# The first feed-forward chunks of a two-layer macaron block: scatters three chunks late, the gate sum on VectorE, new orders

## The chip, the cores and the metric

The kernel runs on one core of one Trainium2 chip. A core has five engines that work side by side, each through its own instructions in order: TensorE (PE in the rows: matrix products; PEld is its weight load), VectorE (DVE), ScalarE (ACT), GpSimd (POOL) and SyncE (SP, which here only issues transfers). They wait for each other on semaphores, and transfers (DMAs) run beside them. The metric is the device time of the program in microseconds (us), the median of three runs. A time is compared at 0.2%, some 4.1 us here.

## The reference, cut to what matters

```python
def _L0_ffn_ref(x, norm_weight, router_w, router_b, fc1_w, fc1_b, fc2_w, fc2_b):
    T, e = b * s, 8;  cap = T // e
    xn = x_flat * rsqrt(mean(x_flat * x_flat) + EPS) * norm_weight
    probs = softmax(xn @ router_w.T + router_b)
    gates, idx = top_k(probs.T, cap)            # every expert picks its cap rows
    hmid = gelu(einsum('ech,efh->ecf', xn[idx], fc1_w) + fc1_b)
    ye = einsum('ecf,ehf->ech', hmid, fc2_w) + fc2_b
    out = zeros.at[flat_idx].add(ye * gates)    # scatter, summed over experts
    gate_sums = zeros.at[flat_idx].add(gates)
    return out / maximum(gate_sums, 1e-9)
x = x + 0.5 * _L0_ffn_ref(_layernorm(x), ...)
x = x + _L0_attn_ref(_layernorm(x), ...)        # causal attention, one head
x = x + 0.5 * _L0_ffn_ref(_layernorm(x), ...)
```

x has 32 x 512 = 16384 rows of 256 numbers; there are 8 experts, each picks 2048 rows and has a hidden width of 1024. All is float32.

## The kernel before, in words

The program goes through router scores, a binary search for each expert's threshold, the first feed-forward layer (layer 0), attention, a second search and the second feed-forward layer (layer 1). Products are made of three float16 products each (`split3`), from a high half (`_h`, made by ScalarE) and a low half (`_l`, made by VectorE).

A feed-forward layer has 32 chunks n of 512 rows, four to an expert (c = n % 4). The text counts chunks from 0. A chunk passes these stations:

- GpSimd gathers its rows from memory (`gather`, four indirect DMAs, one for each block t of 128 rows), and gathers their gate weights (`weights`, four more).
- In layer 0 alone the rows must be normalised: VectorE takes statistics (`rows_stats`, ends in `cx`), GpSimd takes the root (`roots`, `zsx`), VectorE makes the shift (`rows_shift`, `zbx`), ScalarE writes the high half `xs` (`rows_hi`), VectorE the normalised row and the low half (`rows_lo`).
- SyncE turns them by DMA transposes into `xt` (`columns`).
- TensorE makes eight blocks f of the hidden layer (`fc1`, three PSUM banks in turn), ScalarE applies gelu and makes `hid_h`, VectorE `hid_l` (`hidden_lo`), TensorE makes four output blocks t (`fc2`), VectorE adds the bias (`y_bias`, `yb`), ScalarE multiplies by the gate weight (`y_out`, `ys`), and GpSimd adds them to memory by indirect DMAs (`scatter`).

All engines loop over steps m and quarters t. In step m TensorE alternates between two blocks of fc1 of chunk m and one block of fc2 of chunk m - 1. There is no scheduler: the order on each engine is the order of the code, and each engine waits in it. ScalarE in quarter 0 of step m makes two gelus, then `rows_hi(m + 1)`, then goes on with the third gelu, for which TensorE's sixth block (f = 5) waits.

In the first chunks of a layer VectorE still has the choice of rows for experts 1 to 7 to finish (`choice_1` to `choice_8`, in `first_turns`), GpSimd makes the gates and their sums over experts (`gate_sums`, `gates`), and SyncE stores them in memory (`gate_d`), from which `weights` gathers. TensorE makes two small products for the choice (`other_limits`, `other_places`), and a wait of TensorE for VectorE's `choice_7` stands in front of the second. The tables `scaled` and `scattered` say in which step a chunk's `y_out` and scatter stand: from step 5 on both handle chunk m - 1.

## Time and profile before

| | us |
|---|---|
| median of 3 runs | 2062.29 (2060.1 to 2063.11) |
| the profiled execution | 2063.0 |
| its span in the trace | 2061.1 |
| TensorE busy | 1961.4 (95%) |
| VectorE busy | 1452.7 (70%) |
| ScalarE busy | 1399.2 (68%) |
| GpSimd busy | 1260.2 (61%) |

The profiled execution's own time lies 1.9 us above its span and 0.7 us above the median. In a row of the timeline the number in brackets is how long the engine stood idle before the instruction, and behind the arrow is what ended the wait.

### The profile page before, as it was taken

The page shows a single profiled execution, that of the slowest core. Times are in us where ns is not written, and L with a number is a line of the kernel's source. Part 1 is how long each engine was busy: PE and PEld are TensorE (multiplying, and loading weights), DVE is VectorE, ACT ScalarE, POOL GpSimd, SP SyncE. Part 2 cuts the span into 40 slices and gives each one's busy share as a digit, 9 for nine tenths or more (in the row PEclk, how much of TensorE's full clock was granted, in tenths as well). Part 3 has the DMA queues.
Part 4 walks back from the last instruction along what each step waited for, and adds up shares of the span by engine and source line. Part 5 has one row for each costly group of instructions (what it writes and reads, how often), then busy time and mean ns, then how long its engine had stood idle before and what let it go on. Part 6 is the DMA issues. An engine that isn't in the chain of part 4 may idle for free. (4 is left out here: it accounts for less than half of the span.)

```text
span 2061.1 us, 42656 instructions
## 1 busy us (share of the span) xinstructions
PE 1961.4 (95%) x15442; PEld 1360.4 (66%) x15442; DVE 1452.7 (70%) x4301; ACT 1399.2 (68%) x2680; POOL 1260.2 (61%) x1438
## 2 busy tenths in 40 slices
PE   8858999999999999799999999779999999999997
PEld 6635666666666666577777777535666666666665
DVE  7788777677777765488899998787565555656542
ACT  8636666766767776578888787555676676676663
POOL 8234877777777776644444442027877676767674
PEclk9979999999999999999999999989999999999999
DMA  9943555646465544556555553234655464646442
GB/s 289 349 128 93 116 95 96 103 91 131 85 109 93 101 71 70 118 126 160 159 160 164 136 150 109 93 82 104 108 119 100 92 107 88 132 85 108 70 79 35
DMA packets 361746, 242.34 MB, mean 118 GB/s; under 512 B 228929, under 2 KB 348993, under 8 KB 361281
## 3 DMA queue, kind: packets, MB, share of 16 engines
q1 hardware_dynamic: 304192, 172.34, 31.8%
q0 software_dynamic: 57344, 67.29, 21.6%
q8 instruction: 122, 2.00, 0.4%
q14 instruction: 88, 0.71, 0.1%
HBM read 121.03 MB, written 84.93 MB: 100 GB/s over the span
## 5 line engine op out<-in xcount | busy, mean ns | idle before, releaser
L1272 DVE SCALAR_TENSOR_TENSOR hid_l<-hf,hid_h 128x512 f16<-128x512 f32 x512 | 352.4, 700 | 339.8 <-ACT hid_h L718 338.5
L1493 PE MATMUL ps<-w_h,hid_h 128*128 128x256 f16 x2048 | 559.5, 273 | 0.0
L1494 PE MATMUL ps<-w_l,hid_h 128*128 128x256 f16 x2048 | 559.4, 273 | 0.0
L1495 PE MATMUL ps<-w_h,hid_l 128*128 128x256 f16 x2048 | 559.3, 273 | 0.0
L1493 PE MATMUL ps<-xt,w_h 128*128 128x512 f16 x1024 | 390.6, 381 | 16.8 <-ACT hf L819 15.5
L819 ACT ACTIVATE hf<-ps,b 128x512 f32<-128x512 f32 x512 | 345.4, 675 | 75.7 <-PE ps L1495 69.3
L1495 PE MATMUL ps<-xt,w_l 128*128 128x512 f16 x1024 | 390.6, 381 | 0.0
L1494 PE MATMUL ps<-xt,w_h 128*128 128x512 f16 x1024 | 390.5, 381 | 0.0
L718 ACT ACTIVATE ys<-yb,weight 128x256 f32<-128x256 f32 x256 | 128.0, 506 | 340.6 <-DVE yb L1290 335.6
L718 ACT ACTIVATE hid_h<-hf 128x512 f16<-128x512 f32 x512 | 322.5, 630 | 16.3
L605 POOL DMA_INDIRECT weight<-gate_d,gate_at x256 | 258.2, 1009 | 84.0 <-issue 76.8
L615 POOL DMA_INDIRECT out<-ys,tok x128 | 206.7, 1615 | 112.9 <-ACT ys L718 80.3
L1493 PEld LDWEIGHTS ps<-w_h,hid_h 128*128 128x128 f16 x2048 | 201.0, 98 | 50.7 <-issue 0.8
L1494 PEld LDWEIGHTS ps<-w_l,hid_h 128*128 128x128 f16 x2048 | 200.9, 98 | 50.5 <-issue 0.8
L615 POOL DMA_INDIRECT x_d<-ys,tok x128 | 206.7, 1615 | 37.4 <-issue 36.7
L1495 PEld LDWEIGHTS ps<-w_h,hid_l 128*128 128x128 f16 x2048 | 200.8, 98 | 23.5
L595 POOL DMA_INDIRECT xe<-z_d,tok x128 | 138.1, 1079 | 90.6 <-issue 90.3
L595 POOL DMA_INDIRECT xe<-x,tok x128 | 132.4, 1034 | 99.2 <-DVE gate_at L1227 61.2
L1495 PEld LDWEIGHTS ps<-xt,w_l 128*128 128x128 f16 x1024 | 100.7, 98 | 122.3 <-issue 2.8
L1493 PEld LDWEIGHTS ps<-xt,w_h 128*128 128x128 f16 x1024 | 100.7, 98 | 114.0 <-ACT hf L819 17.5
L1494 PEld LDWEIGHTS ps<-xt,w_h 128*128 128x128 f16 x1024 | 100.6, 98 | 94.3 <-issue 1.9
L1290 DVE TENSOR_TENSOR yb<-ps,b_now 128x256 f32<-128x256 f32 x256 | 107.6, 420 | 62.1 <-PE ps L1495 61.1
(292 smaller groups left out, 3848.7 us busy)
## 6 DMA issues: line engine op xcount, KB each, us to landing
w_st<-fc_t SPq DMA_DIRECT2D x32, 1024.0 KB, 6.3
xin<-x SPq DMA_DIRECT2D x32, 512.0 KB, 5.6
xa<-x_d SPq DMA_DIRECT2D x32, 512.0 KB, 4.5
out<-x SPq DMA_DIRECT2D x32, 512.0 KB, 5.2
z_d<-z SPq DMA_DIRECT2D x32, 512.0 KB, 6.0
xt<-xs SPq DMA_TRANSPOSE x256
weight<-gate_d,gate_at POOLq DMA_INDIRECT x256, 2.8
b_st<-fc_b SPq DMA_DIRECT2D x16, 128.0 KB, 5.7
```

What stands on the lines that cost most here:

```text
L595: pool.indirect_dma_start(xe[:, n % 2, t, :], None, rows, bass.IndirectOffsetOnAxis(ap=tok[:, E % 3, k:k + 1].bitcast(U32), axis=0)).then_ ...
L605: pool.indirect_dma_start(weight[:, E % 3, k:k + 1], None, gate_d, bass.IndirectOffsetOnAxis(ap=gate_at[:, E % 3, k:k + 1].bitcast(U32), a ...
L615: pool.indirect_dma_start(acc, bass.IndirectOffsetOnAxis(ap=tok[:, E % 3, k:k + 1].bitcast(U32), axis=0), ys[:, n % 2, t, :], None, comput ...
L718: return act.activation(dst, src, ACT.Copy, **kw)
L819: act.activation(hf[:, f % HF, :], bank(FC1[f % 3]), ACT.Gelu, bias=b1[:, e, f:f + 1], scale=1.0 / WS).then_inc(s_gelu, 1)
L1272: dve.scalar_tensor_tensor(hid_l[:, n % 2, f, :], hf[:, f % HF, :], HS, hid_h[:, n % 2, f, :], ALU.mult, ALU.subtract).then_inc(s_hl, 1)
L1290: dve.tensor_tensor(yb[:, n % 2, t, :], bank(4 + t % 2)[:, 0:D], b2_now[:, n // NC % 2], ALU.add).then_inc(s_yb, 1)
L1493: pe.matmul(dst, lh, rh, start=first, stop=False)
L1494: pe.matmul(dst, lh, rl, start=False, stop=False)
L1495: return pe.matmul(dst, ll, rh, start=False, stop=last)
```

## The change

- SyncE: expert 1's `w2_in` is issued before the gates are stored, and the store moves behind it.
- GpSimd: the four additions of the gate sum go; the product `gate = equal * p_r` stays (`chosen`). The order of gathers, roots, weights and scatters of the first chunks is another. The scatter of chunk n comes four steps late (n = m - 4), from step 13 on three, from step 18 on two, from step 24 on one; so steps 12, 17 and 23 hold two scatters each. `weights` of chunk m - 1 stands in step m (before: of chunk m).
- VectorE: sums the gates over experts by one reduction (`gate_scale`), which reads `gate` with a step of 128 numbers. The parts of the choice, the statistics and the count of slots stand in other places; from step 4 on `rows_stats(m + 2)` stands in quarter 2, not 3.
- ScalarE: in chunks 2 and 3 of layer 0 it writes the normalised row as well (`NORMED`), and VectorE's copy of that work goes. `y_out` handles chunk m - 2 until step 22, two chunks in step 23, then m - 1.
- The halves of the attention's weights are made within the first search (ScalarE rounds 6 to 9, VectorE rounds 8, 10, 11 and 13), no longer in the first chunks.
- The output buffer `ys` has four places instead of two (the new two lie where `above` and `scan` of the choice are).
- TensorE: `pick(E0, 3)` moves from step 1 to step 0, `other_limits` from quarter 0 to quarter 1 of step 1.

The diff, cut:

```diff
+    YS_RING = 4
+    LOWS = (8, 10, 11, 13)
+    NORMED = (2, 3)
...
+        LATE = 23
+
         def scaled(m, t):
...
+            if m < 3:
+                return []
+            if m in (3, LATE):
+                two = 2 * (t % 2)
+                return [((0 if m == 3 else m - 2) + t // 2, two), ((0 if m == 3 else m - 2) + t // 2, two + 1)]
+            return [(m - 2, t)] if m < LATE else [(m - 1, t)]
+
+        def weighted(m):
+
+            return [m - 1] if m < LATE - 3 else [m - 1, m] if m == LATE - 3 else [m]
 
         def scattered(m):
 
-            return {2: [0], 3: [1], 4: [2, 3]}.get(m, [m - 1])
+            lag = 4 if m < 13 else 3 if m < 18 else 2 if m <= LATE else 1
+            return [m - lag, m - lag + 1] if m in (12, 17, LATE) else [m - lag]
...
-                sp.wait_ge(s_gate, layer + 1)
-                sp.dma_start(gate_d..., gate[:, :, :]).then_inc(s_gate_d, 16)
                 w2_in(E0 + 1)
                 for m in range(1, LAST):
                     n, ahead = N0 + m, (N0 + m) // NC + 2
+                    if m == 2:
+                        sp.wait_ge(s_gate, layer + 1)
+                        sp.dma_start(gate_d..., gate[:, :, :]).then_inc(s_gate_d, 16)
...
-                roots(N0 + 2)
-                gate_sums(layer)
                 gather(N0 + 3)
+                chosen(layer)
+                roots(N0 + 3)
                 gates(layer)
-                roots(N0 + 3)
+                gather(N0 + 4)
                 pool.wait_ge(s_gate_d, 16 * (layer + 1))
                 weights(N0)
+                roots(N0 + 4)
                 weights(N0 + 1)
+                gather(N0 + 5)
+                weights(N0 + 2)
+                roots(N0 + 5)
...
-                for m in range(2, LAST + 1):
+                for m in range(4, LAST + 1):
                     if m + 2 < LAST:
                         gather(N0 + m + 2)
+                    late = m >= 12
+                    if not late:
+                        for n in scattered(m):
+                            scatter(N0 + n)
+                        if m + 2 < LAST:
+                            roots(N0 + m + 2)
+                    for n in weighted(m):
+                        if n < LAST:
+                            weights(N0 + n)
+                    if late and m + 2 < LAST:
                         roots(N0 + m + 2)
...
-                            act.activation(xs[:, t, 0, :], xe[:, n % 2, t, :], ACT.Identity, ...)
+                            for dst in (xs[:, t, 0, :], xe[:, n % 2, t, :])[0:2 if n in NORMED else 1]:
+                                last = act.activation(dst, xe[:, n % 2, t, :], ACT.Identity, ...)
...
-                link(dve.tensor_scalar(ginv[:, :], gsum[:, 0, :], 1e-9, None, ALU.max))
+                link(dve.tensor_reduce(ginv[:, :], gate[:, :, :].rearrange("p e t -> p t e"), AX.X, ALU.add))
+                link(dve.tensor_scalar(ginv[:, :], ginv[:, :], 1e-9, None, ALU.max))
...
-                    if (m, t) == (0, 0):
+                    if (m, t) == (0, 1):
+                        choice_2(layer)
+                    if (m, t) == (0, 3):
                         choice_3(layer)
-                    if (m, t) == (0, 2):
                         choice_4(layer)
                     if (m, t) == (1, 0):
+                        count_slots(0, E0, 3)
+                    if (m, t) == (1, 1):
                         choice_5(layer)
-                    if (m, t) == (1, 1):
                         choice_6(layer)
...
                     if (m, t) == (1, 2):
                         choice_7(layer)
+                        rows_stats(E0 * NC + 3)
...
-                        if t == 3 and m + 2 < LAST:
+                        if t == (3 if m < NC else 2) and m + 2 < LAST and m != 1:
                             rows_stats(n + 2)
```

SyncE, from chunk 1's transposes to chunk 3's in layer 0 (and the same in layer 1). `w_st` of L413 is expert 1's second weight matrix, `gate_d` the stored gates. Before:

```order
L420 DMA_TRANSPOSE xt<-xs 128x4x128 x8
L408 DMA w_st<-fc_t 128x2x1024
L420 DMA_TRANSPOSE xt<-xs 128x4x128 x4
L434 DMA gate_d<-gate 128x8x128
L413 DMA w_st<-fc_t 128x8x256
L414 DMA b_st<-fc_b 128x256
L420 DMA_TRANSPOSE xt<-xs 128x4x128 x4
```

The same place in the changed kernel, where L430 is the load of the second matrix and L455 the store:

```order
L437 DMA_TRANSPOSE xt<-xs 128x4x128 x8
L425 DMA w_st<-fc_t 128x2x1024
L437 DMA_TRANSPOSE xt<-xs 128x4x128 x4
L430 DMA w_st<-fc_t 128x8x256
L431 DMA b_st<-fc_b 128x256
L455 DMA gate_d<-gate 128x8x128
L437 DMA_TRANSPOSE xt<-xs 128x4x128 x4
```

The load of the second matrix has moved ahead of the store, which waits for the gates.

GpSimd in layer 0, from the first product of the gates to chunk 5's roots. `xe` rows are gathers, `weight` rows the gathers of gate weights, `zsx` the roots, `x_d<-ys` the scatters. Before:

```order
L571 TENSOR_TENSOR gate<-equal,p_r 128x1024
L572 TENSOR_TENSOR gsum<-gate 128x512
L575 TENSOR_TENSOR gsum<-gsum 128x256
L577 TENSOR_TENSOR gsum<-gsum 128x128
L595 DMA xe<-x,tok 128x256 x4
L581 TENSOR_TENSOR gate<-gate,ginv 128x1024
L622 TENSOR_TENSOR zsx<-cx,minus_half 128x4
L605 DMA weight<-gate_d,gate_at 128x1 x8
L595 DMA xe<-x,tok 128x256 x4
L605 DMA weight<-gate_d,gate_at 128x1 x4
L622 TENSOR_TENSOR zsx<-cx,minus_half 128x4
L615 DMA x_d<-ys,tok 16384x256 x4
```

In the changed kernel, from chunk 3's gather on:

```order
L607 DMA xe<-x,tok 128x256 x4
L589 TENSOR_TENSOR gate<-equal,p_r 128x1024
L634 TENSOR_TENSOR zsx<-cx,minus_half 128x4
L593 TENSOR_TENSOR gate<-gate,ginv 128x1024
L607 DMA xe<-x,tok 128x256 x4
L617 DMA weight<-gate_d,gate_at 128x1 x4
L634 TENSOR_TENSOR zsx<-cx,minus_half 128x4
L617 DMA weight<-gate_d,gate_at 128x1 x4
L607 DMA xe<-x,tok 128x256 x4
L617 DMA weight<-gate_d,gate_at 128x1 x4
L634 TENSOR_TENSOR zsx<-cx,minus_half 128x4
L607 DMA xe<-x,tok 128x256 x4
```

Chunk 3's gather now stands ahead of the product, the three rows of sums are gone, and no scatter stands in this stretch.

GpSimd in layer 0, where the lag of the scatters first shrinks (step 12). Before, a step like every other:

```order
L595 DMA xe<-x,tok 128x256 x4
L605 DMA weight<-gate_d,gate_at 128x1 x4
L622 TENSOR_TENSOR zsx<-cx,minus_half 128x4
L615 DMA x_d<-ys,tok 16384x256 x4
L595 DMA xe<-x,tok 128x256 x4
```

In the changed kernel:

```order
L607 DMA xe<-x,tok 128x256 x4
L617 DMA weight<-gate_d,gate_at 128x1 x4
L634 TENSOR_TENSOR zsx<-cx,minus_half 128x4
L627 DMA x_d<-ys,tok 16384x256 x8
L607 DMA xe<-x,tok 128x256 x4
```

Eight scatter DMAs instead of four stand ahead of the next chunk's gather; this is so again in steps 17 and 23.

## Rows read from the trace of the kernel before

**Rows 1.** Windows: length, busy PE, PEld, DVE, ACT, POOL; PEclk, DMA, GB/s.
```profile
187.59:214.48 26.89, 23.13 (x154) 15.11 (x154) 22.17 (x58) 14.75 (x26) 18.93 (x17) 0.94 0.52 151
214.48:235.77 21.29, 21.29 (x155) 14.52 (x153) 16.84 (x56) 14.65 (x27) 17.38 (x15) 1.00 0.55 86
235.77:263.88 28.11, 23.33 (x154) 14.72 (x152) 18.37 (x59) 14.80 (x27) 22.84 (x19) 0.94 0.52 107
1400.37:1429.16 28.79, 23.99 (x154) 15.46 (x154) 20.57 (x44) 14.00 (x26) 19.29 (x17) 0.88 0.56 147
```

**Rows 2.** Timeline of TensorE where it restarts: start, length, instruction, [idle before <-releaser].
```profile
187.34 0.39 PE L1627 MATMUL ps<-per_expert,before 128*128 128x7 f32 x2 [1.44 <-DVE per_expert L1181]
...
203.44 0.39 PE L1493 MATMUL ps<-xt,w_h 128*128 128x512 f16 x1 [3.76 <-ACT hf L819]
...
251.94 0.61 PE L1493 MATMUL ps<-xt,w_h 128*128 128x512 f16 x1 [3.48 <-ACT hf L819]
...
1417.27 0.61 PE L1493 MATMUL ps<-xt,w_h 128*128 128x512 f16 x1 [4.80 <-ACT hf L819]
```

**Rows 3.** Timeline of ScalarE before those restarts.
```profile
197.92 2.08 ACT L810 ACTIVATE xs<-xe,zbx,zsx 128x256 f16<-128x256 f32 x4 [6.20 <-DVE zbx L1258]
...
249.23 2.08 ACT L810 ACTIVATE xs<-xe,zbx,zsx 128x256 f16<-128x256 f32 x4 [8.53 <-DVE zbx L1258]
...
1416.01 0.63 ACT L718 ACTIVATE w_h<-w_st 128x512 f16<-128x512 f32 x1 [7.66 <-DMA w_st<-fc_t]
```

**Rows 4.** Timeline of SyncE's queue in layer 1.
```profile
1408.33 0.37 SPq L434 DMA_DIRECT2D gate_d<-gate  x1
```

**Rows 5.** Timeline of GpSimd in step 3 of layer 0: chunk 5's roots.
```profile
247.32 1.62 POOL L622 TENSOR_TENSOR zsx<-cx,minus_half 128x4 f32<-128x4 f32 x1
```

**Rows 6.** Timeline of VectorE in the first search and in steps 0 to 2.
```profile
103.71 0.29 DVE L1105 TENSOR_REDUCE got<-ps 128x2 f32<-128x128 f32 x1 [0.36 <-PE ps L1593]
...
145.92 0.75 DVE L979 SCALAR_TENSOR_TENSOR g_l<-ps,g_h 128x256 f16<-128x256 f32 x2
...
170.95 1.89 DVE L1264 TENSOR_SCALAR xe<-xe,zsx,zbx 128x256 f32<-128x256 f32 x4 [0.73 <-ACT xs L810]
...
194.11 1.41 DVE L1247 BATCH_NORM_STATS2 bstx<-xe 128x6 f32<-128x256 f32 x4 [1.39 <-DMA xe<-x,tok]
...
197.66 0.16 DVE L1258 SCALAR_TENSOR_TENSOR zbx<-mvx,zsx 128x4 f32<-128x4 f32 x1
```

**Rows 7.** Groups by line, VectorE's reductions: out<-in, shapes xcount | busy us, mean ns | idle before.
```profile
L1162 DVE TENSOR_REDUCE per_expert<-above 128x7 f32<-128x896 f32 x2 | 2.2, 1079 | 0.0
```

**Rows 8.** Groups by line, GpSimd, 300 to 800 us (24 steps of layer 0).
```profile
L615 POOL DMA_INDIRECT x_d<-ys,tok x96 | 153.8, 1602 | 26.8 <-issue 26.8
L595 POOL DMA_INDIRECT xe<-x,tok x94 | 97.2, 1034 | 28.6 <-issue 28.6
L605 POOL DMA_INDIRECT weight<-gate_d,gate_at x96 | 97.1, 1012 | 29.2 <-issue 29.2
L622 POOL TENSOR_TENSOR zsx<-cx,minus_half 128x4 f32<-128x4 f32 x24 | 27.2, 1135 | 41.9 <-DVE cx L1252 41.9
```

**Rows 9.** Transfers: issues by line, median us from issue to landing.
```profile
weight<-gate_d,gate_at POOLq DMA_INDIRECT x256, 2.8
...
xe<-x,tok POOLq DMA_INDIRECT x128, 2.9
```

**Rows 10.** Timelines of one undisturbed step of layer 0, which begins at 348.14.
```profile
348.14 0.38 PE L1493 MATMUL ps<-xt,w_h 128*128 128x512 f16 x1
...
354.99 2.06 ACT L810 ACTIVATE xs<-xe,zbx,zsx 128x256 f16<-128x256 f32 x4
...
360.08 0.38 PE L1493 MATMUL ps<-xt,w_h 128*128 128x512 f16 x1
...
365.29 0.42 DVE L1290 TENSOR_TENSOR yb<-ps,b_now 128x256 f32<-128x256 f32 x1
...
368.76 0.69 DVE L1272 SCALAR_TENSOR_TENSOR hid_l<-hf,hid_h 128x512 f16<-128x512 f32 x1 [0.55 <-ACT hid_h L718]
```

More of the change, by code:

```diff
@@ L189, in macaron @@
         p_r = sb("p_r", [P, NE, P], F32, ffn)
-        above = sb("above", [P, NE, P], F32, ffn)
         equal = sb("equal", [P, NE, P], F32, ffn)
-        scan = sb("scan", [P, NE, P], F32, ffn)
+        choice = ExitStack()
+        above = sb("above", [P, NE, P], F32, choice)
+        scan = sb("scan", [P, NE, P], F32, choice)
+        choice.close()
+        ys_more = sb("ys_more", [P, 2, TG, D], F32, ffn)
         w1_h = sb("w1_h", [P, 2, KD, FF], F16, ffn)
@@ L297, in macaron @@
         s_xe = [sem("s_xe0"), sem("s_xe1")]
-        s_sc = [sem("s_sc0"), sem("s_sc1")]
+        s_sc = [sem(f"s_sc{u}") for u in range(YS_RING)]
         s_xt = [sem("s_xt0"), sem("s_xt1")]
@@ L665, in ffn_rows @@
                         scatter(m - 1, 2, TG)
-                    else:
-                        for n in scattered(m)[len(early):]:
+                    elif late:
+                        for n in scattered(m):
                             scatter(N0 + n)
@@ L706, in _ @@
             ffn_rows(1, z_d, outf)
-            for u in range(2):
-                pool.wait_ge(s_sc[u], 16 * TG * NC * NE)
+            for u in range(YS_RING):
+                pool.wait_ge(s_sc[u], 16 * TG * (2 * NC * NE // YS_RING))
             pool.sem_inc(s_phase, 1)
@@ L724, in _, with attention_weights @@
             last.then_inc(s_split, 1)
-            def attention_weights():
-                act.wait_ge(s_gm, 2 * KD)
-                for n, dst in enumerate((g_h, m_h)):
-                    for k in range(KD):
-                        last = copy(dst[:, k, :], bank(4 + n)[:, k * D:(k + 1) * D], scale=WS)
-                last.then_inc(s_gmh, 1)
+            def attention_weights(n, k):
+                act.wait_ge(s_gm, KD * (n + 1))
+                copy((g_h, m_h)[n][:, k, :], bank(4 + n)[:, k * D:(k + 1) * D], scale=WS).then_inc(s_gmh, 1)
             def high(g, k):
@@ L773, in route @@
                         act.activation(junk_a[:, :], key, ACT.Sign, bias=at[:, 2:3], scale=-1.0, accum_out=signs[:, 2:3]).then_inc(s_signs, 1)
+                    if layer == 0 and 6 <= i < 6 + 2 * KD:
+                        attention_weights((i - 6) // KD, (i - 6) % KD)
                     if i == 2:
@@ L850, in ffn @@
                     w2_hi(E0, h)
-                if layer == 0:
-                    attention_weights()
                 rows_hi(N0)
@@ L1102, in route @@
                             router_columns(rounds // 3 - 1)
+                        if layer == 0 and rounds in LOWS:
+                            attention_weights(LOWS.index(rounds) // KD, LOWS.index(rounds) % KD)
                         rounds += 1
@@ L1220, in count_slots @@
                 if q == 0:
-                    for u in range(2):
-                        wait(dve, s_sc[u], 16 * TG * (NC // 2) * (E - 2))
+                    for u in range(YS_RING):
+                        wait(dve, s_sc[u], 16 * TG * (NC // YS_RING) * (E - 2))
                     for c in range(NC):
@@ L1260, in rows_lo @@
                 def rows_lo(n, t0=0, t1=TG):
-                    if layer == 0:
+                    if layer == 0 and n not in NORMED:
                         for t in range(t0, t1):
@@ L1333, in ffn @@
                     w1_lo(E0, 1)
+                b2_rows(E0)
                 rows_shift(N0, 2, TG)
-                if layer == 0:
-                    b2_rows(E0)
                 rows_lo(N0, 2, TG)
-                if layer == 1:
-                    b2_rows(E0)
+                count_slots(0, E0, 2)
                 choice_1(layer)
-                count_slots(0, E0, 2)
-                if layer == 0:
-                    router_halves()
-                    attention_weights()
-                choice_2(layer)
-                for h in range(4):
+                w2_lo(E0, 0)
+                rows_stats(N0 + 1)
+                for h in range(1, 4):
                     w2_lo(E0, h)
-                rows_stats(N0 + 1)
                 for m in range(LAST + 1):
@@ L1689, in ffn @@
                             pick(ahead, 2 * c + t // 2)
[L1690 removed]
+                        if (m, t) == (0, 3):
+                            pick(E0, 3)
+                        if (m, t) == (1, 1):
                             other_limits(layer)
[L1692 removed]
                         if (m, t) == (1, 3):
```

63 lines of the change are left out of this document (23 added, 40 removed).

## The prediction, made before the changed kernel was run

> **What bounds the kernel now.** I first read the busy rows of the page: TensorE works 95% of the span, so a change can win only where it stands still or runs at its lower clock. The windows of single chunks show where [rows 1]: a normal step with two `pick` products takes 21.29 us at a granted clock of 1.00 and TensorE is busy throughout. In layer 0 step 2 takes 26.89 us and step 4 takes 28.11; in layer 1 step 2 takes 28.79. These three steps lose 5.60, 6.82 and 7.50 us. The timeline of TensorE gives the stall inside each: 3.76, 3.48 and 4.80 us, all released by a gelu of ScalarE [rows 2]; the remainder is the clock, granted at 0.94, 0.94 and 0.88 of full in those windows, so at the lower level, 1.2 GHz, for some us after each stall. The first matmul after the last two stalls takes 0.61 us where one at full clock takes 0.38 [rows 2, 10]. A shorter stall of 1.44 us stands at the end of step 1, for VectorE's `choice_7` [rows 2].
>
> The timeline of ScalarE says what the gelu stood behind [rows 3]. In layer 0 step 2, `rows_hi(3)` waited 6.20 us for VectorE's shift. In step 4, `rows_hi(5)` waited 8.53 for a shift whose root GpSimd made at 247.32, behind chunk 1's scatters [rows 5]. In layer 1 step 2, the copy of expert 1's second matrix waited 7.66 us for its load, which SyncE issues only behind the store of the gates at 1408.33 [rows 4].
>
> **The change, part by part.** *Layer 1.* The load now stands ahead of the store and is free to go when chunk 2's transposes are out, in step 1, almost a step earlier, which covers a wait of 7.66 us with room. What is late next is `rows_hi(3)`: its gather now goes out ahead of the product of the gates and the sums, so it has landed. Weights of chunk 0 come after the store and after chunk 4's gather, but `y_out(0)` now stands in step 3 and not at the end of step 2, 20 us later. So the 7.50 us go whole. `other_places` finds `choice_7` done there. Gain: 7.5 us.
>
> *Layer 0, step 4.* Chunk 5's root no longer has a scatter ahead of it, since the first scatter stands in step 4 behind chunk 6's gather. VectorE ends chunk 5's statistics at about the time its quarter 3 ends, 1 us of root follows, and the shift is there about 7.5 us into step 4, before `rows_hi(5)` and 2 us before TensorE would want the third gelu (TensorE's f = 5 begins at 360.08 - 348.14 = 11.9 us into a step [rows 10]). Of the 6.82 us I leave 0.5, for a `pick` whose tiles VectorE makes no earlier than now. Gain: 6.3 us.
>
> *Layer 0, steps 0 to 2.* Here VectorE sets the pace, and it works in order. It sheds the four low halves of the attention's weights, 2 x 0.75 us less the overlap, 1.3 us [rows 6], and chunk 3's statistics no longer wait 1.39 us for a gather [rows 6]. It sheds chunk 2's normalisation, 1.89 us and a wait of 0.73 [rows 6], but gains nothing by that: the low halves of chunk 2 now wait for ScalarE, which makes eight activations at 2.08 / 4 = 0.52 us each [rows 3], 4.2 us in all, and the old pair of passes took about as long. It takes on the sum of 1024 numbers. The nearest row is a reduction of 896 contiguous numbers, 1.08 us [rows 7], so 1.2 us if the step costs nothing, 2.4 if every element costs two; I take 1.2, by the row. The choice's parts now all lie before chunk 2's statistics, which gives back about 0.5. Chunk 3's shift, at 197.66 before [rows 6], comes 1.39 + 1.3 - 1.2 - 0.5 = 1.0 us earlier; `rows_hi(3)` itself takes twice as long (4.2 for 2.08), and the load of the matrix, which ended the stall before, is no longer in the way. TensorE's restart, 203.44 [rows 2], moves to about 202.6: 0.8 us. Its idle time there is still some 3 us, between the 1.44 of step 1 and the 3.48 after which the matmul took 0.61, so the lower clock goes or stays: 5.60 - 3.76 = 1.8 us, of which I take 0.8. Steps 0 to 2 then give 1.6 us, with ends of 0 and 4 (the 1.44 of step 1 may grow, since TensorE gets there sooner than VectorE).
>
> The Trainium skill speaks against this sum (SBUF — State Buffer, "Door 1: The DMA port swizzle"): reads that go to a new 16-byte line with each element pay a penalty, and here the step is 512 bytes. It gives no figure for VectorE. By the rows the sum is 1.2 us; by the rule it is longer, up to the 2.4 taken as the end above, which would leave 0 to 0.4 us of step 2's gain. No row of this kernel has such a step in SBUF, so the trace neither agrees nor disagrees.
>
> *The search.* Each of the four rounds gets one low half of 0.4 us on VectorE, which waits 0.36 us for TensorE in a round [rows 6]. Cost: 0.1 us or less a round, 0.2 in all; at worst 1.6.
>
> *The catch-up steps of layer 0.* This is what the change adds. GpSimd's work in a step is 4 x (1.60 + 0.28) = 7.5 us of scatters, 4 x (1.03 + 0.30) = 5.3 of gathers, 4 x (1.01 + 0.30) = 5.3 of weights and 1.1 of roots [rows 8]: 19.2 of 20.9 to 21.3 us, and it waited 41.9 us for `cx` in 24 steps, 1.75 a step [rows 8], which is the same slack. In steps 12, 17 and 23 eight scatters, 15 us, stand between chunk m + 2's root and chunk m + 3's gather. Times from the start of a step: `yb` of quarter 2 begins at 365.29 - 348.14 = 17.2 [rows 10] and statistics now follow it, 17.6 to 19.6; the root ends at 20.7. Fifteen us of scatters bring GpSimd to 36, the fourth gather is issued at 36 + 3 x 1.33 = 40.1 and lands 2.9 us later [rows 9], at 43.0, which is 22.1 us into the next step. VectorE wants it at 17.6, and waits 4.5 us in front of its last two low halves of the hidden layer. They normally end at 368.76 + 0.69 = 369.45, as the following step begins [rows 10], and fc2 of that chunk needs them after two blocks of fc1, 2.6 us later. Now the statistics end at 24.1 and the two low halves at 25.5, which is 4.6 into the following step. TensorE stands for 2.0 us. With 1.75 us of slack a step the queue has recovered before the next catch-up. Three of them: 6.0 us lost, with ends of 0 (the wait is swallowed) and 10 (3.5 each, with a clock that falls). In layer 1 there are no statistics, gathers run a step ahead, and nothing is lost.
>
> *The weights one step late.* From step 4 to 11 the weights of chunk m - 1 go out behind the root, from 20.9, land at 20.9 + 3 x 1.31 + 2.8 = 27.6, 6.7 us into the next step [rows 8, 9]. There `y_out` waits for them in front of `rows_hi`, which then ends at 6.7 + 0.4 + 2.1 = 9.2, and the third gelu at 9.9, TensorE wants it at 11.9. Before, `rows_hi` began at 354.99 - 348.14 = 6.9 [rows 10], so this costs ScalarE half a us and TensorE nothing. If it came 2 us later than I reckon, it would cost from there on in each of eight steps.
>
> The sum: 7.5 + 6.3 + 1.6 - 0.2 - 6.0 = 9.2 us. The profiled execution's 2063.0 us becomes 2053.8, and the median, 0.7 below it, 2053.1.
>
> **The rivals.** *The catch-ups cost nothing.* If VectorE's wait is shorter than its slack (scatters overlap more tightly than their mean, or the gather lands sooner), the 6.0 us stay: 2047.1. For it: the slack of 2.6 us is more than half of the wait. Against it: the arithmetic has 15 us in front of a gather that had 7.5.
>
> *Only SyncE's move pays.* VectorE stays the bound of layer 0's first chunks, the strided sum takes 2.4 us, the lower clock stays, and catch-ups and late shifts take back what step 4 gives: 7.5 - 2.5 = 5 us, 2057.3. For it: VectorE was busy 22.17 of 26.89 us in step 2, which leaves little [rows 1].
>
> *GpSimd's queue becomes the bound of layer 0.* Place: steps 4 to 22 of layer 0, the loop cx, root, weights, `y_out`, `rows_hi`, third gelu. It decides from the point where the weights land 2 us later than reckoned, for example when scatters at four steps' lag meet gathers in the transfer queues and a step of GpSimd grows from 19.2 to over 21 us. At 2 us beyond that point, eight steps cost 16 us, and 16 - 9.2 = 7 us are lost: 2069. For it: GpSimd's slack is 1.75 us a step and the slack of the gelu 2.0. Against it: the work of a step is the same as before.
>
> *It does not do what it says.* The waits are there but another one ends at the same time (the transposes, the ring of four `hf` tiles): within 2 us of before, 2061.
>
> **How the numbers follow.** Forecast 2053.1 with 0.42, its own range 2050 to 2057. Catch-ups free 0.24 (2047.1), only the load 0.18 (2057.3), GpSimd's queue the bound 0.09 (2069), nothing gained 0.07 (2061). The range that holds the time 8 times in 10 takes in the first three: 2045.5 to 2060.5. A measurement of this kernel tells 0.2%, 4.1 us, from no change. Faster by more than that (under 2058.2): the first two and two thirds of the third, 0.78. Within it: a third of the third and the last, 0.14. Slower: 0.08.
>
> **What would show it.** In layer 1, step 2 should take 21.3 us with no wait of ScalarE for `w_st`. In layer 0, step 4 should take under 22 us; step 2 about 25 to 26, with a wait for `zbx` still in it; and the timeline of VectorE should show waits of 3 to 5 us for `xe` in steps 13, 18 and 24, each with a stall of TensorE of about 2 us released by `hid_l`. The reduction into `ginv` should take 1.2 us. Wrong it would be if steps 5 to 12 are longer than 20.9 to 21.3 us, or if TensorE stands still at a place that this text does not name.

## The result, and the profile after

| | before | after |
|---|---|---|
| median, 20 runs each | 2062.24 us (2059.19 to 2067.44) | 2067.96 us (2064.89 to 2072.9) |
| profiled execution, its span | 2063.0, 2061.1 | 2065.61, 2063.5 |
| GpSimd busy | 1260.2 us | 1275.5 us |

The changed kernel is slower: ratio 1.0028, 95% interval 1.0022 to 1.0034. Its profiled execution was one of its quickest (2065.61 against a median of 2067.96), so the two traces differ by 2.4 us where the medians differ by 5.7. The traces account for those 2.4.

The windows of single steps, columns as in [rows 1]: layer 0's steps 2, 8, 14, 19 and 25, and layer 1's step 2.

```profile
186.61:216.03 29.42, 23.88 (x155) 15.00 (x154) 24.52 (x55) 16.06 (x28) 12.00 (x9) 0.88 0.30 88
322.22:344.99 22.77, 21.45 (x154) 14.46 (x152) 16.96 (x48) 13.61 (x24) 15.72 (x13) 1.00 0.66 123
452.18:476.89 24.71, 22.69 (x147) 14.82 (x145) 18.64 (x54) 16.33 (x29) 20.12 (x18) 0.93 0.54 109
561.14:584.03 22.89, 21.01 (x146) 14.00 (x144) 16.03 (x44) 13.88 (x24) 18.64 (x16) 1.00 0.43 72
689.57:713.55 23.98, 21.47 (x155) 14.45 (x153) 17.07 (x62) 14.68 (x25) 19.17 (x17) 1.00 0.42 75
1409.21:1430.71 21.50, 21.45 (x155) 14.44 (x154) 20.91 (x44) 13.53 (x24) 8.32 (x6) 1.00 0.40 73
```

Two of the three long steps of [rows 1] are gone: layer 1's step 2 takes 21.50 us (28.79 before), layer 0's step 4 takes 21.93 (28.11). Step 2 of layer 0 got longer, 29.42 for 26.89. Steps 8, 14, 19 and 25, which took 21.29, 20.84, 20.84 and 21.29 before, have become long.

The timeline of TensorE after, its restarts in those steps and in step 12; one later matmul shows the clock.

```profile
204.58 0.61 PE L1513 MATMUL ps<-xt,w_h 128*128 128x512 f16 x1 [5.41 <-ACT hf L842]
339.56 0.38 PE L1686 MATMUL ps<-counts,tile_of 128*128 128x128 f16 x4 [1.32 <-DVE tok_f L1240]
425.46 0.38 PE L1686 MATMUL ps<-counts,tile_of 128*128 128x128 f16 x4 [1.49 <-DVE tok_f L1240]
456.96 0.28 PE L1513 MATMUL ps<-w_h,hid_h 128*128 128x256 f16 x1 [2.02 <-DVE hid_l L1294]
461.06 0.57 PE L1513 MATMUL ps<-xt,w_h 128*128 128x512 f16 x1
565.77 0.28 PE L1513 MATMUL ps<-w_h,hid_h 128*128 128x256 f16 x1 [1.88 <-DVE hid_l L1294]
694.84 0.28 PE L1513 MATMUL ps<-w_h,hid_h 128*128 128x256 f16 x1 [2.51 <-DVE hid_l L1294]
```

Three causes stand behind these rows. *Steps 14, 19, 25*: VectorE waits for the gather that stands behind eight scatters, in steps 13, 18 and 24.

```profile
453.62 1.41 DVE L1269 BATCH_NORM_STATS2 bstx<-xe 128x6 f32<-128x256 f32 x4 [6.25 <-DMA xe<-x,tok]
562.50 1.41 DVE L1269 BATCH_NORM_STATS2 bstx<-xe 128x6 f32<-128x256 f32 x4 [5.94 <-DMA xe<-x,tok]
691.56 1.41 DVE L1269 BATCH_NORM_STATS2 bstx<-xe 128x6 f32<-128x256 f32 x4 [5.18 <-DMA xe<-x,tok]
```

*Steps 8 and 12*: the weights land late, so ScalarE (first row, step 8) makes the high half late, VectorE (second row) waits for it, and everything behind it on VectorE is late, last `tok_f`, which TensorE's `pick` waits for.

```profile
329.86 0.51 ACT L740 ACTIVATE ys_more<-yb,weight 128x256 f32<-128x256 f32 x1 [3.50 <-DMA weight<-gate_d,gate_at]
330.89 1.89 DVE L1286 TENSOR_SCALAR xe<-xe,zsx,zbx 128x256 f32<-128x256 f32 x4 [2.77 <-ACT xs L832]
```

*Step 2*: VectorE's timeline, and GpSimd's two products beside it. The last row is chunk 3's shift.

```profile
181.66 4.25 DVE L1200 TENSOR_TENSOR_SCAN scan<-equal 128x896 f32<-128x896 f32 x1
192.13 1.90 DVE L1215 TENSOR_REDUCE ginv<-gate 128x128 f32<-128x1024 f32 x1
195.46 3.44 DVE L1294 SCALAR_TENSOR_TENSOR hid_l<-hf,hid_h 128x512 f16<-128x512 f32 x2
199.16 0.14 DVE L1280 SCALAR_TENSOR_TENSOR zbx<-mvx,zsx 128x4 f32<-128x4 f32 x1
```

```profile
181.65 2.36 POOL L589 TENSOR_TENSOR gate<-equal,p_r 128x1024 f32<-128x1024 f32 x1
195.63 2.73 POOL L593 TENSOR_TENSOR gate<-gate,ginv 128x1024 f32<-128x1024 f32 x1 [5.89 <-DVE ginv L1218]
```

The shift was at 197.66 [rows 6] and the step began 0.98 later than now, so within the step it is 2.5 us later. The scan took 2.21 us before, and the two low halves in this place 1.28:

```profile
196.05 1.28 DVE L1272 SCALAR_TENSOR_TENSOR hid_l<-hf,hid_h 128x512 f16<-128x512 f32 x2
```

Step by step from the starts of the fc1 blocks, the account of the traces (gain positive): all ahead of layer 0's first fc1, the search included, +0.85; step 0 +2.28; step 1 -2.15; step 2 -2.53; step 4 +6.18; steps 8 and 12 -1.48 and -1.65; steps 14, 19, 25 -3.87, -2.05, -2.69; step 28 -0.39; from the start of layer 0's last chunk to the fc1 of layer 1 (attention and the second search lie there) -1.78; layer 1's steps 0 and 1 together +0.44, step 2 +7.29; from the start of its last chunk to the end -0.85. Sum -2.4.

### The profile page after: what moved, and what is told of

Its sections match the earlier page's. It is cut to its first block, busy times and chain, and to the rows that moved or that the text cites. A ratio compares the mean times of both kernels' runs of the same rounds, so it can differ in the third digit from the quotient of the medians.

```text
span 2063.5 us, 42662 instructions
## 1 busy us (share of the span) xinstructions
PE 1958.3 (95%) x15442; PEld 1357.8 (66%) x15442; DVE 1453.5 (70%) x4295; ACT 1403.1 (68%) x2688; POOL 1275.5 (62%) x1432
## 4 chain that ended last, share of the span: by engine, by line
PE 65%; POOL 12%; issue 9%; DVE 7%; ACT 4%; DMA 2%; SPq 1%; DVEq 0%; POOLq 0%; ACTq 0%
PE ps L1513 20%; PE ps L1515 20%; PE ps L1514 20%; POOL x_d L627 5%; POOL xe L607 3%; POOL weight L617 2%; ACT zt_l L740 2%; PE ps L1739 1%; ACT zt_h L740 1%; PE ps L1613 1%; DVE hid_l L1294 1%; POOL zsx L634 1%; DMA xe<-x,tok 1%; DVE bst L1023 1%; PE ps L1768 1%
## 5 line engine op out<-in xcount | busy, mean ns | idle before, releaser
L607 POOL DMA_INDIRECT xe<-x,tok x128 | 136.7, 1068 | 112.6 <-DVE gate_at L1249 75.3
L627 POOL DMA_INDIRECT out<-ys,tok x64 | 108.1, 1689 | 44.9 <-issue 31.4
L627 POOL DMA_INDIRECT out<-ys_more,tok x64 | 104.9, 1639 | 42.5 <-ACT ys_more L740 26.0
L561 POOL TENSOR_TENSOR nt<-mv,minus_one 128x4 f32<-128x4 f32 x64 | 13.4, 210 | 184.9 <-DVE mv L1027 184.9
```

The lines of the kernel that those rows point to most:

```text
L607: pool.indirect_dma_start(xe[:, n % 2, t, :], None, rows, bass.IndirectOffsetOnAxis(ap=tok[:, E % 3, k:k + 1].bitcast(U32), axis=0)).then_ ...
L627: pool.indirect_dma_start(acc, bass.IndirectOffsetOnAxis(ap=tok[:, E % 3, k:k + 1].bitcast(U32), axis=0), scaled_rows(n)[:, t, :], None, c ...
```

## The experiments

Each kernel was timed beside the kernel before, with 4 to 12 executions of it; e_flat alone has a single one. Line numbers in rows are those of the kernel named. What a step took beyond its undisturbed 21.29 or 20.84 us, from the starts of the fc1 blocks in each trace, steps 2 to 30 of both layers, under 0.2 us left out. A step is read from one execution of each kernel, and that one can be among its quickest or slowest (the ratio is from all of them). Steps 0 and 1 are not in the table: step 1 of layer 0 takes 23.3 us in before, a_load, b_root, x_ring, x_root and y_chosen, and 25.0 to 27.0 in the others.

| kernel | layer 0: step and us lost | layer 1 | ratio to before (95%) |
|---|---|---|---|
| before | 2: 5.6, 4: 6.8 | 2: 7.5 | 1 |
| after | 2: 8.1, 4: 0.6, 8: 1.5, 12: 1.6, 14: 3.9, 19: 2.1, 25: 2.7, 28: 0.4 | 2: 0.2 | 1.0028 (1.0022 to 1.0034) |
| a_load | 2: 4.8, 4: 6.9 | 2: 0.6, 5: 7.7 | 1.0008 (0.9999 to 1.0018) |
| b_root | 2: 5.9, 4: 0.7, 5: 5.1, 8: 4.4 | 2: 7.0, 5: 1.3 | 1.0015 (1.0006 to 1.0024) |
| f_two | 2: 6.4, 4: 0.7, 5: 6.4 | 2: 0.6, 5: 7.7 | 1.001 (1.0001 to 1.0019) |
| x_ring | 2: 6.6, 4: 0.7, 5: 4.3 | 2: 0.6, 6: 1.4 | 0.998 (0.997 to 0.9989) |
| x_root | 2: 6.6, 4: 0.7, 6: 4.9, 10: 0.3, 20: 4.3 | 2: 0.6, 6: 2.0 | 0.9977 (0.9967 to 0.9986) |
| c_catch | 2: 7.5, 4: 0.7, 8: 1.5, 12: 1.7, 15: 6.0, 20 to 26: 4.7, 28: 0.4 | 2: 0.2 | 1.0025 (1.0012 to 1.0038) |
| d_weights | 2: 8.6, 4: 0.7, 14: 4.4, 19: 4.1, 25: 4.3 | 2: 0.2 | 1.0021 (1.0012 to 1.003) |
| s_spread | 2: 7.7, 4: 0.7, 8: 0.9, 12: 2.2 | 2: 0.2 | 0.9981 (0.9972 to 0.999) |
| e_scale | 2: 12.6, 3: 2.8, 4: 0.6, 8, 12: 3.1, 14, 19, 25: 9.7 | 2: 8.1, 3: 1.9 | 1.012 (1.0105 to 1.0136) |
| g_scale | 2: 2.0, 4: 0.7, 8, 12: 3.2, 14, 19, 25: 9.8, 28: 0.3 | 2: 0.8 | 1.0004 (0.9992 to 1.0015) |
| t_all | 2: 12.6, 3: 2.7, 4: 0.6, 23: 0.7, 28: 0.4 | 2: 8.1, 3: 1.9 | 1.0035 (1.0023 to 1.0047) |
| w_best | 2: 2.0, 3: 0.8, 28: 0.6 | 2: 0.8 | 0.9931 (0.9919 to 0.9944) |
| y_chosen | 2: 3.9, 4: 0.6, 28: 0.2 | 2: 0.8 | 0.9931 (0.9918 to 0.9944) |

### Parts of the change put into the kernel before

**a_load.**

```diff
                 columns(N0 + 2)
-                sp.wait_ge(s_gate, layer + 1)
-                sp.dma_start(gate_d..., gate...).then_inc(s_gate_d, 16)
                 w2_in(E0 + 1)
                 for m in range(1, LAST):
...
+                    if m == 2:
+                        sp.wait_ge(s_gate, layer + 1)
+                        sp.dma_start(gate_d..., gate...).then_inc(s_gate_d, 16)
```

> The kernel before with one edit: in both layers SyncE issues the load of expert 1's second matrix ahead of the store of the gates, and the store stands where the changed kernel has it. My theory: this alone is worth what layer 1's step 2 lost, 7.5 us, so 2054.7 us (ratio to before 0.9964); step 2 of layer 1 takes about 21.5 us and ScalarE has no wait for w_st. Rival: in the kernel before chunk 3's gather still stands behind the gate sums on GpSimd, and a wait for it or for weight takes the place of the one removed: 2 to 4 us gained only, 2059, and step 2 at 25 us. Layer 0 gains nothing in either.

Measured 2064.55 us: nothing gained. Step 2 of layer 1 lost only 0.6, as both theories of its own step allow, but step 5 took 28.96 us. ScalarE's and TensorE's rows there:

```profile
1478.31 0.51 ACT L719 ACTIVATE ys<-yb,weight 128x256 f32<-128x256 f32 x1 [10.14 <-DMA out<-ys,tok]
1480.67 0.61 PE L1494 MATMUL ps<-xt,w_h 128*128 128x512 f16 x1 [4.69 <-ACT hf L820]
```

ScalarE waits 10.14 us for a buffer that a scatter still reads. In this trace and in that of before GpSimd works from 1413 to 1489 with no pause but the 0.3 us between two issues. So the scatters of chunk 2, for which ScalarE waits, are out only 2.6 us sooner (the last is issued at 1474.51, before at 1477.10), while TensorE begins step 5 at 1463.88 instead of 1471.74. Without the stall of step 2 TensorE comes to them sooner than they are done: there the stall had been the time in which GpSimd drew level. Neither theory had this.

**b_root.**

```diff
-                    early = scattered(m)[:1] if m in (3, 4) else []
+                    early = scattered(m)[:1] if m == 4 else []
```

> The kernel before with one edit: in step 3 GpSimd makes chunk 5's root ahead of chunk 1's scatters, not behind them; ring of two output buffers, everything else as before. My theory: step 4 of layer 0 (28.11 us) falls to 22 to 23, 5 to 6 us gained, ratio 0.9973, and the four output buffers and the three-step lag were not needed for it. Rival: with two buffers the scaling of chunk 3 waits for chunk 1's scatters, now 1.4 us later, and the stall of step 4 stays in another place: 0 to 2 us gained, ratio 0.9995.

Measured 2065.86 us. Step 4 fell to 22.00 us, as the theory has it, and step 5 rose to 26.39 and step 8 to 25.67, so nothing is gained: the rival's wait for a scatter came, a step later than it said. In step 5 a root behind the next scatters (VectorE waits 5.22 us for it) and a scatter behind them are late together; in step 8 ScalarE waits 4.74 us for weights. ScalarE and TensorE in step 5:

```profile
269.60 0.51 ACT L718 ACTIVATE ys<-yb,weight 128x256 f32<-128x256 f32 x1 [8.39 <-DMA x_d<-ys,tok]
272.70 0.61 PE L1493 MATMUL ps<-xt,w_h 128*128 128x512 f16 x1 [3.53 <-ACT hf L819]
```

**f_two** has both edits.

> The kernel before with both small moves, SyncE's load ahead of the store and chunk 5's root ahead of chunk 1's scatters, ring of two. Theory (GpSimd's backlog): the stalls come back as they did with each move alone, in step 5 and 8 of layer 0 (5.1 and 4.4 us) and step 5 of layer 1 (7.7 us), so nothing is gained: ratio 1.000 to 1.002. Rival: the two moves together gain what each took out of its own step, 6 + 7, ratio 0.994.

Measured 2064.86 us. Step 5 of layer 1 loses the same 7.7 us, step 5 of layer 0 loses 6.4, step 8 nothing: the first theory holds but for step 8.

**x_ring** is f_two with `YS_RING = 4` and `scaled_rows` taken over from the change, `scaled` and `scattered` left alone.

> As f_two, and four output buffers in place of two, with scaling and scatters where the kernel before has them (no lag, no catch-up). Theory: with two buffers ScalarE waits 8 to 10 us for a scatter in step 5; four buffers take that wait away, so step 5 of both layers is 21.3 us and the gain stays: layer 1 gives 7, layer 0 gives 6, less up to 4.4 in step 8 where ScalarE waits for weight: ratio 0.994 to 0.9965. Rival: GpSimd is late by its own work, and the next thing behind it (root, gather or weight) is late by as much in steps 5 to 8 whatever the ring: ratio 0.999 to 1.001.

Measured 2057.89 us, a ratio between those of theory and rival. Layer 1 is as the theory has it: step 5 takes 21.28 us, and only 1.4 come back, in step 6. In layer 0 step 5 still takes 25.54, and the wait there is not for a scatter now. VectorE's row:

```profile
268.81 0.16 DVE L1267 SCALAR_TENSOR_TENSOR zbx<-mvx,zsx 128x4 f32<-128x4 f32 x1 [5.79 <-POOL zsx L631]
```

**x_root** sets `early = []` as well, so that every root stands ahead of the scatters.

> As x_ring, and chunk 6's root too ahead of the scatter of step 4, so that in every step the root stands ahead of the scatters; scaling and scatters are as early as in the kernel before. Theory: what stayed in x_ring (step 5 of layer 0 at 25.5 us) is VectorE's wait of 5.8 us for that root, behind chunk 2's scatters; it goes, and step 5 is 21.3 us: 4.2 us less than x_ring, 2053.7, ratio to before 0.996. Then neither the lag of three steps nor the catching up was needed. Rival: GpSimd's own backlog still makes gathers or weights late in steps 5 to 8, at least 3 of the 4 us come back there: ratio 0.9975 or more.

Measured 2059.33 us. Step 5 takes 21.29, and step 6 takes 25.73: the wait is now VectorE's, for a gather.

```profile
286.85 1.41 DVE L1256 BATCH_NORM_STATS2 bstx<-xe 128x6 f32<-128x256 f32 x4 [5.65 <-DMA xe<-x,tok]
```

The rival holds. This trace, that of the slowest of the kernel's 11 executions, also has a stall of TensorE of 2.47 us in step 20 that x_ring's lacks: ScalarE waits 4.67 us there for weights, and `tok_f` is late behind it; why the weights came late is open. With prompt scatters GpSimd's backlog costs 4 to 7 us somewhere in steps 4 to 6 of layer 0 (before, b_root, f_two, x_ring, x_root), whichever wait is moved. In the changed kernel, with its lag, steps 5 to 7 are undisturbed, and they stay so in g_scale and w_best, below, where step 2 no longer gives GpSimd time. Up to and with its work for step 4 GpSimd makes the scatters of four chunks in the kernel before and of one in the changed kernel, some 22 us less. This speaks for the lag, but no run takes the lag alone out of the change or puts it alone into the kernel before; the sums that GpSimd sheds and its new order could have a share.

### Parts of the change taken back or mended

**c_catch.**

```diff
-                    if m + 2 < LAST:
+                    if m + 2 < LAST and len(scattered(m - 1)) == 1:
                         gather(N0 + m + 2)
...
                         for n in scattered(m):
                             scatter(N0 + n)
+                            if len(scattered(m)) == 2 and n == scattered(m)[0]:
+                                gather(N0 + m + 3)
```

> The changed kernel with one edit: in steps 12, 17 and 23 the gather of chunk m + 3 stands between the two scatters and not behind both. My theory: the waits of VectorE for xe in steps 13, 18 and 24 (6.25 us in step 13) and the stalls of TensorE behind them (2.02, 1.88, 2.51 us and the lower clock after the first) go; steps 14, 19 and 25 of the changed kernel are 3.9, 2.1 and 2.7 us too long, so 7.5 to 8.5 us come back: ratio to before 0.9989 (after: 1.0028). Rival: eight scatters fill GpSimd for 15 us wherever the gather stands, so weights or scatters are late instead, and only a third comes back: 1.0015.

Measured 2068.84 us, no better than the changed kernel. Step 14 is undisturbed and step 15 loses 6.0:

```profile
475.66 1.41 DVE L1271 BATCH_NORM_STATS2 bstx<-xe 128x6 f32<-128x256 f32 x4 [6.92 <-DMA xe<-x,tok]
478.93 0.40 PE L1515 MATMUL ps<-w_h,hid_h 128*128 128x256 f16 x1 [2.85 <-DVE hid_l L1296]
```

The gather after the one I had saved was late. The rival's reason holds (eight scatters are too much for a step), and not even its third came back.

**s_spread.**

```diff
+        EXTRA = (8, 13, 23)
...
         def scattered(m):
-            lag = 4 if m < 13 else 3 if m < 18 else 2 if m <= LATE else 1
-            return [m - lag, m - lag + 1] if m in (12, 17, LATE) else [m - lag]
+            def quarters(m):
+                return TG * (m - 3) + sum(min(max(m - a + 1, 0), TG) for a in EXTRA)
+            return [divmod(q, TG) for q in range(quarters(m - 1) if m > 4 else 0, quarters(m))]
...
-                        for n in scattered(m):
-                            scatter(N0 + n)
+                        for n, t in scattered(m):
+                            scatter(N0 + n, t, t + 1)
```

> The changed kernel with one edit: GpSimd makes up the three steps of lag not with eight scatters in each of steps 12, 17 and 23, but with one tile's scatter more in each of steps 8 to 11, 13 to 16 and 23 to 26. Theory: a step of GpSimd has about 1.75 us free and one more scatter is 1.9 us, so the queue stays within a fraction of a us; the waits for xe and the stalls of steps 13, 14, 19 and 25 go and with them 8.6 us (3.9 + 2.1 + 2.7), ratio to before 0.9986; steps 8 and 12 keep their 1.5 and 1.65. Rival: GpSimd is full anyway, so four steps with 1.9 us more each bring the same stall once at their end: 1.0015 or worse.

Measured 2059.14 us, ratio 0.9981 where the changed kernel has 1.0028. Steps 13 to 27 are all undisturbed. VectorE still waits for `xe` in several of them, 2.25 us at most, and its slack hides that. The trace is that of the quickest of 11 executions, 5.7 us under their median, so a typical one may lose more than it shows; the ratio, from all of them, gives a gain of 9.7 us.

**d_weights** makes `weights(m - 1)` stand ahead of `scatter(m - 4)` in layer 0's steps 4 to 11.

> The changed kernel with one edit: in layer 0, steps 4 to 11, GpSimd asks for the weights ahead of the scatters and not behind the root. My theory: steps 8 and 12 of the changed kernel are 1.5 and 1.65 us too long because ScalarE waits 3.5 and 3.9 us for weight, VectorE waits 2.8 and 3.2 for ScalarE's halves and makes the tiles late; these waits go and 3.1 us come back: ratio 1.0013. Rival: the root now stands at the end of the queue and comes later, so that the shift is late and steps 5 to 12 are all longer: 1.003 or more. Second rival: the tiles are late because the statistics stand in quarter 2, and nothing changes: 1.0028.

Measured 2066.03 us. Steps 8 and 12 take 21.28 and 21.29 us: the cause is as said, and both rivals are out. But steps 14, 19 and 25 lost 12.8 us here and 8.6 in the trace of after, with stalls that differ little (2.56, 2.25 and 2.43 us for 2.02, 1.88 and 2.51): the windows of the three steps show a clock of 0.93 each, where those of after show 0.93, 1.00 and 1.00. By the ratios 1.4 us of the 3.1 remain, which this measurement cannot tell from nothing.

**e_flat** changes only what is added up: `rearrange("p (t e) -> p t e")`.

> The changed kernel, with the reduction into ginv over 8 neighbouring numbers of the tile in place of numbers 128 apart (so the gates are divided by another sum; nothing else differs). It prices the stride: the strided one takes 1.90 us in the changed kernel. If the stride costs, it falls to about 1.2 us; if 128 short sums cost what they do whatever the stride, it stays at 1.9.

```profile
192.36 1.21 DVE L1215 TENSOR_REDUCE ginv<-gate 128x128 f32<-128x1024 f32 x1
```

So the stride costs 0.7 us of the 1.90 (in layer 1 the two take 1.21 and 1.94). By the Trainium skill (SBUF — State Buffer, "Door 1: The DMA port swizzle") each access that crosses to a new 16-byte line pays a penalty; these two rows agree in direction. Step 2 did not get shorter for it (29.46 us). Otherwise this kernel does in time what the changed one does, and it shows how far one execution is from another: steps 14 to 25 lose 13.2 us in its trace, 8.6 in that of after.

**e_scale.**

```diff
                     if (m, t) == (1, 3):
...
-                        gate_scale(layer)
...
+                    if (m, t) == (2, 1):
+                        gate_scale(layer)
```

> The changed kernel with one edit: VectorE makes the sums and the reciprocals of the gates (gate_scale) not at the end of step 1 but in step 2 behind chunk 3's shift and low halves. Theory: VectorE's order up to chunk 3's shift sets the restart of TensorE in step 2. 3.3 us of gate_scale and 2.2 us by which GpSimd's product stretched the low halves of the hidden layer go from in front of it: step 2 falls from 29.4 to 22.5 to 24.5 us, 5 to 7 us gained, ratio 0.9998. Rival: GpSimd is what bounds layer 0 from here, so a shorter step 2 only brings a wait for weight or scatter in steps 3 to 5: less than 2 us gained, 1.0022.

Measured 2086.57 us, my worst miss here. The shift came at 194.54, earlier as planned. But GpSimd could begin the product with `ginv` only at 209.17, and SyncE sends chunk 3's transposes behind the store of the gates. Rows of SyncE, then TensorE:

```profile
212.51 0.37 SPq L455 DMA_DIRECT2D gate_d<-gate  x1
212.97 5.89 SPq L437 DMA_TRANSPOSE xt<-xs  x4
```

```profile
221.35 0.61 PE L1514 MATMUL ps<-xt,w_h 128*128 128x512 f16 x1 [11.86 <-DMA xt<-xs]
```

**g_scale** puts it between the shift and the low halves instead.

```diff
                     if (m, t) == (1, 3):
...
-                        gate_scale(layer)
...
                             rows_shift(n + 1)
+                            if m == 2:
+                                gate_scale(layer)
                             rows_lo(n + 1)
```

> The changed kernel with one edit: gate_scale between chunk 3's shift and its low halves in step 2 (the edit of w_best alone). Theory: what the change lost in steps 0 to 2 is VectorE's order: 3.3 us of gate_scale and the 2.2 us by which GpSimd's product stretches the low halves of the hidden layer stand in front of chunk 3's shift. Step 2 falls from 29.4 to 23.3 us as in w_best, the rest of the changed kernel stays (steps 8, 12, 14, 19, 25 too long): 6 us less than the changed kernel, ratio to before 0.9999. Rival: a step 2 that is 6 us shorter gives GpSimd 6 us less before the weights of steps 5 to 12 and the first catching up, so steps 8, 12 and 14 grow by 3 us or more in all: ratio 1.0014 or more.

Measured 2062.95 us, 5.0 below the changed kernel. Step 2 takes 23.31 us. Steps 8, 12, 14, 19 and 25 lose 13.0 where they lost 11.7. The theory holds, and by the ratios this one place is worth 5.0 of the 5.8 us between the two kernels (the interval of g_scale's ratio is 2.4 us to either side).

**t_all** joins s_spread, d_weights and e_scale.

> The changed kernel with three edits together: scatters spread (as s_spread), weights ahead of the scatters in layer 0's steps 4 to 11 (as d_weights), gate_scale behind chunk 3's shift (as e_scale). If the three causes are separate, the gains add: 8.6 + 3.1 + 6 = 17.7 us from 2068, so 2050, ratio to before 0.9942. If GpSimd's queue is the common bound, the stalls move: 2058 to 2062, ratio 0.998 to 1.000, with a stall of TensorE in steps 3 to 6 or at the end of the spread.

Measured 2069.71 us; neither expectation came true, since both took e_scale for a gain. It carries e_scale's fault (12.6 and 2.7 us in steps 2 and 3, 8.1 and 1.9 in layer 1). Of steps 5 to 30 only 23 and 28 are disturbed, by 0.7 and 0.4 us.

**w_best** joins s_spread, d_weights and g_scale.

> The changed kernel with three edits: scatters spread (s_spread), weights ahead of the scatters in layer 0's steps 4 to 11 (d_weights), and gate_scale between chunk 3's shift and its low halves, so that GpSimd and SyncE get the gates at about the time they do now. Theory: s_spread's 2059.1, less 0.9 and 2.2 for steps 8 and 12, less 4.5 to 6 for step 2 (29.0 us there, 23 to 24.5 here): 2050.5, ratio 0.9943. Rival: the gates are again late at GpSimd or at SyncE and chunk 3's transposes wait behind the store: step 2 or 3 as long as before or longer, ratio 0.997 or more.

Measured 2047.81 us (2045.67 to 2052.05), ratio 0.9931, interval 0.9919 to 0.9944: 14.8 us below the kernel before and, by the ratios, 20 below the changed one. It also beats the theory's 2050.5. Its VectorE at chunk 3's shift:

```profile
193.24 0.15 DVE L1287 SCALAR_TENSOR_TENSOR zbx<-mvx,zsx 128x4 f32<-128x4 f32 x1
193.31 1.92 DVE L1222 TENSOR_REDUCE ginv<-gate 128x128 f32<-128x1024 f32 x1
196.65 3.58 DVE L1297 TENSOR_TENSOR xs<-xe,xs 128x256 f16<-128x256 f32 x4
```

**y_chosen** is w_best with `roots(N0 + 3)` ahead of `chosen(layer)`.

> w_best with one edit more: GpSimd makes chunk 3's root ahead of the product of the gates, so that the product no longer runs beside VectorE's scan (4.25 us in the changed kernel, 2.21 in the kernel before). Theory: the scan falls to 2.2 us and the stall of 2.19 us at the end of step 1 with it; 1 to 2 us less than w_best in each layer where it counts, ratio 0.9935. Rival: the product stretches counts, tiles or the low halves instead and the shift comes no earlier: same as w_best.

Measured 2048.59 us, the same ratio. The scan fell to 2.01 us, and `counts` took 3.00 us (1.09 in the kernel before), because the product now ran beside it:

```profile
181.85 2.01 DVE L1207 TENSOR_TENSOR_SCAN scan<-equal 128x896 f32<-128x896 f32 x1
187.98 3.00 DVE L1217 TENSOR_TENSOR counts<-scan,per_expert 128x889 f16<-128x889 f32 x1
```

The rival holds: the shift stands at 193.54 where w_best has it at 193.24. Step 1 of layer 0 fell from 25.52 us to 23.27 as the theory wanted, and step 2 gave it back, 25.20 for 23.29.

## Why the prediction was wrong, point by point

- *Layer 1, 7.5 us.* Measured 7.7 in steps 0 to 2. The number was right and its reason half: I gave it to SyncE's move and asked no more of GpSimd than that chunk 3's gather and chunk 0's weights be in time. a_load shows that the move by itself gains nothing, since 7.7 us come back in step 5. The four buffers had to be there too: with them (x_ring) only 1.4 us come back. What in the change saves these, no run tells apart. That the changed kernel had what it took was luck as far as the prediction goes, which reckons with no return.
- *Layer 0, step 4, 6.3 us.* Measured 6.2. The mechanism was right for step 4, but b_root and x_root show that a root ahead of the scatters by itself only sends the loss on to step 5 or 6; the prediction does not have that. In the changed kernel it stays away, most likely by the lag, which is argued and not shown.
- *Layer 0, steps 0 to 2, 1.6 us gained.* This step failed: 2.4 lost (67.30 us from the first fc1 to step 3 before, 69.70 after). Chunk 3's shift was to come 1.0 us earlier and came 1.5 later on the clock of the trace. The reduction took 1.90 us for 1.2. The larger part is a term that the sum does not have at all, GpSimd's products of the gates beside VectorE's instructions: against the kernel before 2.0 us more on the scan and 2.2 on the two low halves of the hidden layer, 4.2 in all. The kernel before had paid 1.1 us of that kind, on the low halves at 181.98, which is gone, so 3.1 net. g_scale shows the remedy: with `gate_scale` behind the shift, step 2 loses 2.0 us and not 8.1.
- *The weights one step late, 0.* This step failed too, by 3.1 us. I had the arrival within 1 us (6.7 into the step; step 8's `y_out` ran 7.6 into it) and followed it to the third gelu, which indeed was in time. I did not follow it on VectorE: low halves, then the tiles, then `tok_f`, which `pick` waits for in steps 8 and 12. d_weights shows it.
- *The catch-ups, 6.0 us with ends of 0 and 10.* The mechanism came true, step by step: the gather landed 22.7 us into step 13 (22.1 forecast), the low halves ended 4.7 into step 14 (4.6), TensorE stood 2.02, 1.88 and 2.51 us (2.0 each). Only VectorE's wait was longer, 6.25 us for 4.5, since it came to it 1.1 us earlier than reckoned. The term was mis-sized: 8.6 in this trace, because the first stall was followed by the lower clock (the matmul of 0.57 us at 461.06, the window at 0.93), worth 1.85, and the third was longer. In the traces of e_scale, g_scale, d_weights and e_flat, which catch up in the same way, the term is 9.7, 9.8, 12.8 and 13.2, and by the ratios s_spread gained 9.7 by doing without it.
- *The search, 0.2 lost.* No loss was seen; layer 0 began 0.85 us earlier. That is no gain of the change either: layer 0's first fc1 begins at 145.0 to 147.4 us in all sixteen traces, with the old search and with the new.
- *Not forecast:* 0.4 in step 28, whose cause stays open; 1.8 between layer 0's end and layer 1's fc1, a stretch that takes 554.0 to 558.7 us in the sixteen traces (556.2 before, 558.0 after), so that nothing can be read from it; and 0.85 behind the start of layer 1's last chunk. This last comes with the four buffers: the stretch takes 42.6 to 42.8 us in before, a_load, b_root and f_two and 43.3 to 43.5 in all kernels with four, and x_ring differs from f_two in nothing else.
- *Signs and medians.* The prediction's own test had it: it called itself wrong if steps 5 to 12 grew or TensorE stood at a place it does not name, and both `pick`s are such. There is also the further distance of 3.1 us between the two profiled executions and the medians (after's 2.35 below its median, before's 0.76 above). The four other traces of the catch-up, with 1.0 to 4.6 us more than after's, suggest that a typical execution of the changed kernel loses more there; that is not shown.

In the traces, then, 9.2 us of gain became 2.4 of loss: 4.0 of the 11.6 between them lie in steps 0 to 2, 3.1 in the late weights, 2.6 in the catch-ups, 3.0 in the places not forecast, and the search gave 1.05 of it back.

The rival on the slower side put the loss into GpSimd's queue through late weights in every step from 4 to 22, 2069. The time is near by luck, the way is not: the late weights cost only in steps 8 and 12.

## What to carry to other kernels

A stall gives every other engine time. When one is removed in front of an engine with little slack (GpSimd's 19.2 of 21 us a step), ask what that engine had left to catch up, and look a few steps on: in a_load, b_root and f_two the loss reappeared there in full, and in x_ring, with more buffers, in part. A lag must then be paid back in pieces of about the slack of a step, one scatter (1.9 us against 1.75) and not four. And follow a late operand on every engine that waits for it, down to the last instruction queued behind.
